# Two cross-attention layers: context turned by transposing DMAs, K split straight from PSUM

## The reference, cut to what matters

```
layer 0 (16 heads of 32), all in float32:
  qn, kn = layer_norm(x), layer_norm(ctx)        # same gain and shift; vn = kn
  Q, K, V = qn @ wq + bq, kn @ wk + bk, kn @ wv + bv
  out = softmax(Q K^T / sqrt(32)) V @ wo + bo;  x = x + out
  x = x + (gelu(layer_norm(x) @ w1 + b1) @ w2 + b2)
layer 1 (16 heads of 64):
  Q, K, V = x @ Wq, ctx @ Wk, ctx @ Wv           # the context is not normalised
  out = softmax(Q K^T / 8 - 0.5*4/4) V @ Wfc + x;  out = layer_norm(out)
```

## Time and profile before

| | |
|---|---|
| median of three runs | 1623.66 us |
| span of the profiled execution | 1604.4 us |
| PE busy | 1418.0 us, 88% |
| DVE busy | 935.5 us, 58% |
| ACT busy | 666.4 us, 42% |
| POOL busy | 431.3 us, 27% |
| DMA queue of SP | 147.34 MB, 33.5% of 16 engines |

### The profile page before, as it was taken

The page is one execution under the profiler, slowest core; times in us unless marked ns, Lnnn a source line. Parts: engine busy times, 40 slices in busy tenths (PEclk is TensorE's granted clock), DMA queues, the critical chain, the costliest instruction groups (busy, mean ns, idle before and its releaser), DMA issues. The chain is left out here.

```text
span 1604.4 us, 34148 instructions
## 1 busy us (share of the span) xinstructions
PE 1418.0 (88%) x12908; PEld 900.5 (56%) x12908; DVE 935.5 (58%) x1677; ACT 666.4 (42%) x1294; POOL 431.3 (27%) x487
## 2 busy tenths in 40 slices
PE   5497898899999756999959999999999999999968
PEld 3255566566656532544435666666666666666653
DVE  5856788798887747622343555454544454555444
ACT  1324565566555534421122444444444444444441
POOL 3212444455443445020000111111111111111124
PEclk9798999999999766999979999999999999999979
DMA  4263333323332033210284333334333333332221
GB/s 139 64 175 103 107 74 103 109 69 107 105 104 64 28 95 112 72 60 27 75 241 105 101 95 75 90 101 102 101 95 84 98 95 81 101 101 65 57 84 65
DMA packets 117005, 149.59 MB, mean 93 GB/s; under 512 B 51056, under 2 KB 92528, under 8 KB 113776
## 3 DMA queue, kind: packets, MB, share of 16 engines
q1 hardware_dynamic: 116848, 147.34, 33.5%
HBM read 71.12 MB, written 22.48 MB: 58 GB/s over the span
## 5 line engine op out<-in xcount | busy, mean ns | idle before, releaser
L642 POOL TENSOR_TENSOR attn_probs<-attn_p,attn_probs 128x400 f16<-128x400 f32 x192 | 188.1, 980 | 915.1 <-ACT attn_probs L993 914.9
L1112 DVE TENSOR_REDUCE attn_nmax<-attn_p_max 100x1 f32<-100x722 f32 x256 | 231.3, 904 | 109.2 <-PE attn_p_max L839 102.8
L817 PE MATMUL attn_p_proj<-attn_ctxT,kv_w_k 128*128 128x361 f16 x1536 | 251.6, 319 | 21.7 <-DMA attn_ctxT<-ctxT_parts 18.2
L822 PE MATMUL attn_p_proj<-kv_w_v,attn_ctxT 128*128 128x512 f16 (+1 forms) x1152 | 264.3, 379 | 0.0
L983 ACT ACTIVATE attn_p<-attn_p_sc,attn_score_bias 128x400 f32<-128x400 f32 x192 | 113.5, 591 | 299.4 <-PE attn_p_sc L868 298.6
L817 PEld LDWEIGHTS attn_p_proj<-attn_ctxT,kv_w_k 128*128 128x128 f16 x1536 | 145.4, 98 | 107.9 <-DMA attn_ctxT<-ctxT_parts 18.6
L993 ACT CAST attn_probs<-attn_p 128x400 f16<-128x400 f32 (+1 forms) x384 | 197.8, 516 | 0.0
L822 PEld LDWEIGHTS attn_p_proj<-kv_w_v,attn_ctxT 128*128 128x128 f16 (+1 forms) x1152 | 110.4, 101 | 111.0
L642 DVE TENSOR_TENSOR attn_probs<-attn_p,attn_probs 128x400 f16<-128x400 f32 (+1 forms) x192 | 119.9, 625 | 89.2 <-ACT attn_probs L993 88.5
L983 ACT ACTIVATE attn_p<-attn_p_sc 128x400 f32<-128x400 f32 x192 | 95.8, 499 | 152.4 <-PE attn_p_sc L864 150.0
L822 PE MATMUL attn_p_proj<-l_w_v,attn_ctxT 128*128 128x512 f16 (+1 forms) x576 | 136.2, 388 | 0.8 <-DVE attn_vbuf L1159 0.8
(11 more groups left out here) (179 smaller groups left out, 2570.6 us busy)
## 6 DMA issues: line engine op xcount, KB each, us to landing
attn_ctxT<-ctxT_parts SPq DMA_DIRECT2D x16, 1444.0 KB, 6.5
attn_kstack_a<-attn_knat SPq DMA_DIRECT2D x128, 180.5 KB, 3.5
attn_kstack<-attn_knat SPq DMA_DIRECT2D x192, 90.2 KB, 2.2
ctxT_parts<-attn_ctxT SPq DMA_DIRECT2D x8, 1444.0 KB, 5.9
attn_kstack_b<-attn_knat SPq DMA_DIRECT2D x64, 180.5 KB, 3.6
attn_c<-in_ctx_dram SPq DMA_DIRECT2D x40, 256.0 KB, 3.2
rows_wo_w<-in_L_xattn_w_dram SPq DMA_DIRECT2D x8, 512.0 KB, 3.6
cols_w_w<-in_L_xattn_w_dram SPq DMA_DIRECT2D x4, 1024.0 KB, 5.5
```

The costliest lines, as they stand in the source:

```text
L642: eng.tensor_tensor(probs[:r, g % 2, 1, t, :HG * SQ], p32[:r, t % 3, :], probs[:r, g % 2, 0, t, :HG * SQ], ALU.subtract).then_inc(p_lo_mad ...
L817: last = pe.matmul(bank[:, :HALF], w_k[:, wa, k, c0 + m * P:c0 + (m + 1) * P], ctxT[:, par, ca, k, n * HALF:(n + 1) * HALF], **flags)
L822: last = pe.matmul(bank[:r, :], ctxT[:, par, ca, k, P * t:P * t + r], w_v[:, wa, k, c0:c0 + E], **flags)
L1112: dve.tensor_reduce(nmax[:SQ, hh:hh + 1], p_max[:SQ, :, :HALF], AX.XY, ALU.max, negate=True).then_inc(max_made, 1)
```

## The change

The context is scaled by 1/std when it is split, so that `ctxT` holds finished rows, and it is turned by DMAs that transpose (`dma_start_transpose`, issued by SP) in both layers; layer 1 loads, splits and turns the context again instead of reading a copy. Gone are the transposes on PE and their copies on DVE, the diagonals and rstd rows, the spill and the reload. K of layer 0 is split straight from PSUM, as in layer 1 (its weights are folded with scale 4 in place of 256, and the query scale is divided by 4). In layer 0 the context's low half moves from POOL to DVE; in layer 1 it is made by POOL (for the first batch by DVE and POOL in turn). `c32` has six buffers in layer 0 and two in layer 1. Rows of a tile are rounded up to a multiple of 16 for the transpose (`TROWS`). SP's program is no longer a loop, and the loop of layer 1's other engines has four steps a round and three rounds, for two steps and seven rounds. `prob_lo` is as before.

```diff
+TROWS = [-(-r // 16) * 16 for r in KROWS]
+SKP = P * (KT - 1) + TROWS[-1]
+KS = 4.0
 # Slots
-        self.ctx = {2: 0, 6: 1, 12: 2, 14: 3, 17: 4, 20: 5} if layer == 0 else {}
-        self.var_t, self.diag_t = 19, 20
-        self.bc = {22: 0, 23: 1} if layer == 0 else {}
+        self.stat = {t: t for t in range(KT)} if layer == 0 else {}
+        self.var_t = KT
+        self.ctx = {8: 0, 10: 1, 12: 2, 14: 3, 16: 4, 18: 5} if layer == 0 else {2: 0, 6: 1, 9: 2}
 # loop of steps
-            with eng.Fori(1, last_loop // 2) as i:
-                for par in range(2):
-                    step(2 * i + par, par, sl.kind(2))
+            with eng.Fori(0, (U - 4) // (2 * per)) as i:
+                for n in range(2, 2 + 2 * per):
+                    step(2 * per * i + n, n % 2, 2 * i + n // per, n // per % 2, sl.kind(2))
 # SP
+            def transpose_ctx(b, t):
+                r = TROWS[t]
+                sp.wait_ge(c_lo_made, b * KT + (t + 1) - (KT if layer else 0))
+                sp.dma_start_transpose(ctxT[:, b % 2, :, :, P * t:P * t + r].rearrange("p a k s -> p (a k) s"),
+                                       cparts[:r, t % 2].rearrange("p a n -> p (a n)")).then_inc(c_moved[t % 2], 16)
 # SP, layer 0
+                def unit(u, prep):
+                    load_q(u, u % 2, u)
+                    stack_k(u, u % 2, 0)
+                    if prep:
+                        for t in range(3):
+                            transpose_ctx(u + 1, t)
+                    stack_k(u, u % 2, 1)
+                    if prep:
+                        for t in range(3, KT):
+                            transpose_ctx(u + 1, t)
+                    if u + 2 < U:
+                        for t in range(KT):
+                            load_ctx_tile(u + 2, t)
                 for t in range(KT):
                     load_ctx_tile(0, t)
+                for t in range(KT):
+                    transpose_ctx(0, t)
+                    load_ctx_tile(1, t)
                 count = 0
                 for m in range(ET):
                     sp.wait_ge(q_lo_made, 2 * m + 2)
                     count += store_queries(sp, q_d, qT, m, q_stored)
 # SP, layer 1
+                def ahead(b, t):
+                    transpose_ctx(b, t)
+                    if t + NC < KT:
+                        load_ctx_tile(b, t + NC)
+                    elif b + 1 < B:
+                        load_ctx_tile(b + 1, t + NC - KT)
+                def unit(u, prep):
+                    load_q(u, u % 2, u // 2)
+                    stack_k(u, u % 2, 0)
+                    if prep:
+                        ahead(u // 2 + 1, 3 * (u % 2))
+                    stack_k(u, u % 2, 1)
+                    if prep:
+                        ahead(u // 2 + 1, 3 * (u % 2) + 1)
+                        ahead(u // 2 + 1, 3 * (u % 2) + 2)
+                for t in range(KT):
+                    load_first(t)
+                for t in range(NC):
+                    load_ctx_tile(1, t)
+                for t in range(KT):
+                    transpose_first(t)
 # PE, before the first projection of a batch
-                        pe.wait_ge(misc_freed, sl.misc_count(u - 1, ("ctx", KT - 1)))
+                    for i in range(2):
+                        pe.wait_ge(c_moved[i], (16 // sl.per) * (KT // 2) * u + 16 * (KT // 2))
 # ACT
             def ctx_hi(b, t):
                 r = KROWS[t]
                 if not (isinstance(b, int) and b == 0 and t < 2):
...
+                    act.wait_ge(c_moved[t % 2], 16 * (KT // 2) * b + 16 * (t // 2))
+                if layer == 0:
+                    act.wait_ge(rstd_made, b + 1)
+                    act.activation(cparts[:r, t % 2, 0, :], c32[:r, t, :], ACT.Identity, scale=rstd[:r, t:t + 1]).then_inc(c_hi_made, 1)
+                else:
+                    act.wait_ge(c_loaded[t % NC], 16 * (KT // NC) * (b - 1) + 16 * (t // NC + 1))
+                    act.copy(cparts[:r, t % 2, 0, :], c32[:r, t % NC, :]).then_inc(c_hi_made, 1)
 # DVE, layer 0, one slot after ctx_hi
+            def ctx_lo(b, t):
+                r = KROWS[t]
+                dve.wait_ge(c_hi_made, b * KT + (t + 1))
+                dve.scalar_tensor_tensor(cparts[:r, t % 2, 1, :], c32[:r, t, :], rstd[:r, t:t + 1], cparts[:r, t % 2, 0, :],
+                                         ALU.mult, ALU.subtract).then_inc(c_lo_made, 1)
 # DVE, K in both layers, after ACT's high half from the same bank
-                        dve.tensor_tensor(kscaled[:, m % 2, cols], p_proj[:, a % 2, :HALF], rrow[:, par, cols],
-                                          ALU.mult).then_inc(proj_freed, 1)
+                    dve.wait_ge(k_hi_made, 8 * u + (a + 1))
+                    shift, op = (kb_col[:, m:m + 1], ALU.add) if layer == 0 else (1.0 / WS, ALU.mult)
+                    dve.scalar_tensor_tensor(knat[:, m, 1, cols], p_proj[:, a % 2, :HALF], shift, knat[:, m, 0, cols],
+                                             op, ALU.subtract).then_inc(proj_freed, 1)
 # ACT before the first step of layer 0, behind each split of a query tile (DVE does the same with ctx_lo)
                 for u in range(2 * ET):
...
+                    if u >= 2:
+                        ctx_hi(0, u - 2)
```

More of the change, by code:

```diff
@@ L512, in kind @@
     def kind(self, s):
-        return (self.layer == 0 and s + 1 < self.units, s < self.units, 1 <= s <= self.units, s >= 2)
+        return (s // self.per + 1 < B if isinstance(s, int) else True, s < self.units, 1 <= s <= self.units, s >= 2)
     def misc_count(self, s, use):
-        before = KT + 2 if self.layer == 0 else 0
+        before = 0
         if isinstance(s, int):
-            if s < 0:
-                return ([("ctx", t) for t in range(KT)] + [("bc", 0), ("bc", 1)]).index(use) + 1
             for q in range(s):
@@ L645, in steps @@
         def steps(eng, step):
[L647 removed]
+            per = sl.per
             for s in range(2):
[L649 to L654 removed]
+                step(s, s % 2, s // per, s // per % 2, sl.kind(s))
+            with eng.Fori(0, (U - 4) // (2 * per)) as i:
+                for n in range(2, 2 + 2 * per):
+                    step(2 * per * i + n, n % 2, 2 * i + n // per, n // per % 2, sl.kind(2))
+            for s in range(U - 2, U + 2):
+                step(s, s % 2, s // per, s // per % 2, sl.kind(s))
         @blk.sync
@@ L770, in _ @@
+            place_onehot()
+            for u in range(U):
+                unit(u, sl.kind(u)[0])
+            load_next_weights(sp)
         @blk.tensor
@@ L845, in max_transposes @@
                 pe.wait_ge(nm_made, G1)
-                misc_wait(s, ("max", g), first=(layer == 1 and isinstance(s, int) and s == 0))
+                misc_wait(s, ("max", g), first=(isinstance(s, int) and s == 0))
                 pe.transpose(misc16[:, :SQ], nmax_parts[:SQ, :], ident16[:SQ, :SQ]).then_inc(misc_ready, 1)
@@ L907, in out_transposes, with step @@
                 last.then_inc(misc_ready, 1)
-            def step(s, par, kind):
+            def step(s, par, b, cpar, kind):
                 prep, proj, has_scores, outs = kind
@@ L1038, in step @@
                             prob_hi(s - 1, *divmod(j - 1, KT))
-                    if prep and j + 2 in sl.ctx:
-                        ctx_hi(s + 1, sl.ctx[j + 2])
-                    if prep and j in sl.bc:
-                        rstd_row(s, par, sl.bc[j])
+                    if prep and j in sl.ctx:
+                        ctx_hi(b + 1, sl.ctx[j] + (3 * par if layer else 0))
                     if outs and j == sl.out_t - 2:
@@ L1177, in out_copy, with step @@
                 dve.tensor_copy(out[:, :, :, bass.ds(b * SQ, SQ)], src).then_inc(misc_freed, 1)
-            def step(s, par, kind, batch=None):
+            def step(s, par, b, cpar, kind):
                 prep, proj, has_scores, outs = kind
@@ L1221, in step @@
                     if proj:
-                        if layer == 0 and j in sl.k_lo:
-                            k_lo(s, sl.k_lo[j])
                         for a in sl.evac[j]:
```

347 lines of the change are left out of this document (110 added, 237 removed).

## The result

The changed kernel takes 1627.55 us, the median of 20 runs (1620.21 to 1632.86), against 1617.07 for 20 runs of the kernel before (1608.59 to 1628.66): a ratio of 1.0055, 95% interval 1.0039 to 1.0071. The forecast was 1613 from a base of 1623.7, so 10.7 us faster; it is 10.5 us slower.

The account below looks back on a forecast made before the run. TensorE bounds layer 1; in layer 0 TensorE and VectorE are both nearly full. Layer 0's steps -26, its start +13, layer 1's start +6, loop heads -3.4 sum to -10: from 1623.7 to 1613 us, range 1588 to 1652.

Parts of the forecast that it names:

- Together 5.0 us on TensorE's own path, from a step of 55.9: Layer 0 steps: removing six tile turns (2.6 us) and two rstd rows shortens TensorE's path by 5.0 us a step.
- VectorE net -5.4 us a step: Layer 0 steps: PSUM copies, diagonals and K work removed, context low halves added; VectorE's work falls 5.4 us from 48.7.
- Rival A: Layer 0 steps: VectorE's relief counts in full, waits for maxima vanish, 8.5 us a step; about 1588 us, chance 0.17.
- ScalarE stands 4 us; I put what the new stand adds at 0.6: Layer 0 steps, slot 18: ScalarE waits 4 us for a transpose to free a buffer, adding 0.6 us a step.
- -26 in the forecast: Layer 0's steps: each falls from 55.9 to 51.5 us, 4.4 a step over six steps, -26 us.
- Layer 0's start: Transposes wait in SP's queue among stores and stacks; step 1 starts near 149.5 instead of 136.44, +13 us.
- Layer 1's start: Loading, splitting and turning the context replaces reading a ready-made copy: first projection later, +6 us.
- zero, hidden by TensorE's 96%: Layer 1's steps: three more splits a unit on ScalarE and GpSimd cost zero, hidden behind TensorE being 96% busy.
- Loop heads: Layer 1's loop: three rounds of four units instead of seven rounds, at 0.84 us of TensorE waiting each, -3.4 us.
- The base: Time of the kernel before, median of three runs: 1623.7 us, 19.3 above the profiled execution's 1604.4.
- B: Rival: a transpose takes 2 us more from issue to landing; steps -14, layer 0's start +20, layer 1's +15; 1641, chance 0.24.
- C: Rival: DMA rings become the bound, 12.2 us a turned tile, deciding from 6.2 us; near 1900 us, chance 0.12.

Follow-up runs that it names:

- unrolled kernel before: The kernel before the change with its attention loops written out in full: 1597.29 us, ratio 0.9883 to the kernel before.
- turns put back: Six-buffer kernel with loops written out, plus TensorE's removed context transposes in layer 0's preparing steps, idle and unread: 1602.87 us, ratio 0.9920 to the kernel before.
- six-buffer kernel: The changed kernel with six buffers in place of two for layer 0's split context tiles: 1608.98 us, ratio 0.9953 to the kernel before.
- unrolled pair: The kernel before and the six-buffer kernel, both with attention loops written out in full: 1597.29 us (0.9883) and 1598.25 us (0.9908).
- 1638.59 kernel: Six-buffer kernel, loops written out, with layer 0's projections, statistics and context splits in other slots and layer 1's second batch loaded behind the first transposes: 1638.59 us, 1.0136.
- one experiment: Layer 0 as in the changed kernel plus a copy of the turned context to DRAM, layer 1 as in the kernel before: 1647.98 us, ratio 1.0202.

## Why the prediction was wrong, point by point

1. **"Together 5.0 us on TensorE's own path, from a step of 55.9": this step failed, and it carried the forecast.** At full clock a step of the unrolled kernel before takes 55.3 us, of which TensorE waits 2.6 for maxima; after, 54.96 and 5.1. TensorE's busy time fell by 3.6 us (51.9 to 48.2); its waits rose by 2.5 for maxima and 1.6 for two new ones and lost one of 0.7: 0.3 us net where 4.4 were forecast. The turns put back cost 0.9 us a step of their 2.5, and the full-clock step with six buffers is 1.1 below that of the unrolled kernel before (54.2 for 55.3): so some 0.2 is left for all else, with the two rstd rows, priced at 2.4, in it. I priced both by their spacing in the timeline, which is what they take, not what the step loses: a slot without a projection is bound by the chain matmul, reduction on VectorE (0.9 us), next matmul.
2. **"VectorE net -5.4 us a step": right as busy time (48.7 to 43.4), worth nothing.** Relieving VectorE by 2.0 us more left the waits at 4.4. TensorE waits for the latency of one maximum, not for VectorE's queue: with a projection ahead of each maximum these waits fell to 0.7. Rival A stood on this and is refuted.
3. **"ScalarE stands 4 us; I put what the new stand adds at 0.6".** It stood 1.8 in slot 18, less than forecast, but the price was too low: TensorE was idle for 1.9 us there, the granted clock was 0.50 for the next 6 us, and the last three of the six steps took 3.2 us more through it (58.2 for 54.96; the first of them holds the loop's head as well). Six buffers remove the stand. The lower clock isn't new with the change: before, TensorE waits 2.5 to 4.1 us for a maximum near the end of four of its six steps, and the clock falls there too. So the steps, -26 in the forecast, are -0.3 in this pair of profiles. By the medians, whose difference of 10.5 holds +10.4 and +11.7 for the starts, they would be some -11.6, if the starts and all other stages are the same in every execution, which is not shown.
4. **Layer 0's start: +13 forecast, +10.4 measured, by the forecast's path.** The first projection began at 89.6 (forecast: last landing at 88), ScalarE waited in slot 12 till 123.5 (125), TensorE 13 us for V's evacuation (19), step 1 began at 147.1 (149.5).
5. **Layer 1's start: +6 forecast, +11.7 measured.** In the steps a landing took 3.2 us (taken 3.5) and an issue 1.27 (0.7). What I left out is that the six are issued one after another behind eight loads, of which two are for the next batch: the first two held SP for 2.2 and 3.6 us and landed after 6.9 and 5.7, and the last was issued at 856.0, 4 us after its data.
6. **Layer 1's steps "zero, hidden by TensorE's 96%": +5 us** in the unrolled pair (706.7 to 711.8), of which 4 are twelve units of 43.4 for 43.0. TensorE's share says that it seldom waits, not that the engine which frees its banks may be late; the split moved to slot 5 made it zero.
7. **Loop heads: -3.4 forecast, -2.1 by TensorE's idle time.** The forecast divided 5.9 us by seven rounds; a loop of seven rounds returns six times, one of three returns twice. TensorE's waits at the heads in layer 1 (total, times, longest), before and after:

```profile
PE attn_p_max L839 <- issue: 5.9, 6, 1.3
```

```profile
PE attn_p_max L821 <- issue: 3.8, 2, 2.0
```

So a return cost 1.0 us with two units in the body and 1.9 with four. With loops in both, points 6 and 7 and all else make +0.1 of layer 1's steps (714.7 to 714.8), where 5 less 2.1 would be +3; the first and the last unit, in part at the lower clock, were 1.3 us shorter after, and the rest isn't accounted for.
8. **The base.** 1623.7 was the median of three and 1617.07 is that of 20, and what lies around a span is 1.8 us, not 19.3: the profiled execution was a short one. The base was 6.6 us too high, which hid a part of the miss: 1613 is 14.5 us too low, the sum of the terms (-10.7 against +10.5) 21. By term: +14.4 for layer 0's steps (points 1 and 3, -26 to -11.6), -2.6 (4), +5.7 (5), +3.5 (6 and 7).

Of the signs that were named: in the steps no landing passed 5.0 us, but an issue held SP for up to 2.9 us, and at layer 1's start one held it for 3.6 and one landing took 6.9; the step at full clock, 54.96, is just below the 55 that would have said wrong, and the mean of the six, 57.7, is above.

Of the rivals, B (1641) comes nearest to the steps' gain (-14; some -11.6 by the medians) and to layer 1's start (+15; +11.7), but by luck: it has them from transposes that land 2 us later, and these landed as the forecast took them; its +20 for layer 0's start is twice what was measured. C is excluded: a transposed tile takes 1.3 us of SP and lands in 3.2, far from 6.2. The estimate from the Trainium skill (DMA: Bandwidth & Descriptors, Latency and other measured facts: 261 GB/s, so 1 us for 256 KB) is less than a third of what the trace shows from issue to landing, 3.2 us. The Trainium skill's page VectorE: DVE Perf Modes (The three transpose paths) gives 1309 ns for a block of 128x128; taken one after another, eight blocks would be 10.5 us, and the trace shows that they don't add up so: 3.2 for all eight.

Not settled: how much of layer 0's difference in the unrolled pair is the clock (a step at full clock takes 55.3 and 54.2 us, six of them 7 us; the other 7 go with steps below it, four of six there and two here, in one execution each); what the rstd rows cost by themselves, which no run put back; why a return to the loop's head costs what it does; and what each of the moved slots did in the 1638.59 kernel.

## What to carry to other kernels

Work taken off the busiest engine is worth its duration only where that engine would not have waited: look at the slots that it leaves behind, and compare them with the chain through the other engines. Buffers that a queued DMA frees need a depth that covers the queue's longest stretch, at the start of a stage above all, where stores, stacks and transposes stand in one line; here four more buffers were worth 1.0%, and another order in the queue nothing. A stage's serial start (load, split, turn with TensorE idle) is best made during the stage before: it was 11 us here, against the 14 that layer 0's steps save in the unrolled pair.

## What the runs showed of the hardware that I had not expected

- A transposing DMA of 128 rows by 1024 float16 from SBUF to SBUF holds SP for 1.27 us in the median (1.2 to 2.9) and lands 2.8 to 5.0 us after its issue, 3.2 in the median, in the steps. Of six issued behind loads still under way, the second held SP for 3.6 us and the first landed after 6.9; with two loads fewer ahead of them, the six took 9.7 us of the queue and not 11.3.
- TensorE's granted clock was 0.50 from 423 to 430 in the changed kernel, around an idle time of 1.9 us behind another of 0.8, and 1.00 again before the next step. In the six-buffer kernel idle times of 0.8 and 1.2 us were followed by some 3 us at 0.50 in one step and not in others: the steps took 54.2 to 54.7 us where it stayed at 1.00 and 56.6 where it fell.
- A return to the head of a hardware loop left TensorE idle for 2.7 us in layer 0 of the kernel before, 3.8 in the changed one and 9.4 in one experiment, all with two steps in the body; in layer 1 for 1.0 with two units in the body and 1.9 with four. Written out, the programs are 0.5% (six buffers) and 1.2% (kernel before) faster.
- How long one small operation of VectorE takes went with what GpSimd did: the low half of a maximum, 100x4 elements, took 162 ns in the six-buffer kernel, 391 in the kernel before and 562 in the one with the context's low half back on GpSimd; GpSimd is busy 19.9, 28.5 and 32.4 us a step there.
